# Turning the quantised codes of a feed-forward tile with a transposing DMA instead of TensorE, from tile 14 on

## The reference

```
# attention without softmax, 16 heads of 16: q = elu(xWq+bq)+1, k = elu(xWk+bk)+1, k /= |k|
scores = einsum('bhqd,bhkd->bhqk', q, k);  attn = einsum('bhqk,bhkd->bhqd', scores, v)
x = layernorm(x + (layernorm(x + attn @ Wo + bo) * gamma + beta))

def fp4_quant_dequant(x):            # blocks of 16 along the last dim
    scale = max(max(abs(xb)) / 6, 1e-12)
    xn = xb / scale                  # rounded to 0, .5, 1, 1.5, 2, 3, 4, 6 with its sign
    return rounded(xn) * scale
def fp4_linear(x, w): return fp4_quant_dequant(x) @ fp4_quant_dequant(w).T
h = silu(fp4_linear(x, w_gate)) * fp4_linear(x, w_up)      # w_gate, w_up: 704 x 256
x = layernorm(x + fp4_linear(h, w_down))                   # w_down: 256 x 704
```

## Time and profile before

| | |
|---|---|
| median of 3 runs (lowest, highest) | 700.19 us (700.13, 703.07) |
| the profiled execution, whole | 700.59 us |
| its span, first to last instruction | 698.9 us |
| outside the span | 1.7 us |
| busy share PE / DVE / ACT / POOL | 98% / 84% / 70% / 87% |

### The profile page before, as it was taken

How to read it: one execution, slowest core, us unless ns; L and a number is a source line. 1 busy time by engine, 2 the same in 40 slices (tenths; PEclk the granted TensorE clock), 3 DMA queues, 4 the chain that set the end, 5 groups by cost and what they waited for, 6 DMA issues and landing times.

```text
span 698.9 us, 14240 instructions
## 1 busy us (share of the span) xinstructions
PE 683.4 (98%) x4370; PEld 602.8 (86%) x4370; DVE 584.1 (84%) x1441; ACT 489.3 (70%) x954; POOL 608.8 (87%) x947
## 2 busy tenths in 40 slices
PE   8999999999989999999999999999999999999995
PEld 6888888888868799999999999999999999999995
DVE  6678678876778899889989998998998998998774
ACT  4677777766777676777677677677767767767664
POOL 3988898988888998899989989899899988989766
PEclk9999999999999999999999999999999999999999
DMA  8544443344301111122211122122111211100001
GB/s 267 189 136 136 136 140 117 131 157 155 107 32 34 58 47 46 45 78 75 76 66 57 36 86 80 57 76 76 46 61 62 77 45 47 61 17 16 21 28 45
DMA packets 23135, 56.36 MB, mean 81 GB/s; under 512 B 2642, under 2 KB 5908, under 8 KB 23060
## 3 DMA queue, kind: packets, MB, share of 16 engines
q1 hardware_dynamic: 22640, 55.32, 23.4%
q10 hardware_dynamic: 420, 0.13, 0.1%
HBM read 30.22 MB, written 25.17 MB: 79 GB/s over the span
## 4 chain that ended last, share of the span: by engine, by line
PE 91%; DVE 2%; POOL 2%; issue 2%; ACT 1%; DMA 1%; SPq 0%; POOLq 0%; DVEq 0%
PE banks L407 23%; PE banks L408 22%; PE banks L409 22%; PE banks L553 8%; PE banks L524 7%; PE banks L445 2%; PE banks L418 2%; PE banks L567 1%; PE banks L566 1%; PE banks L431 1%; PE banks L476 1%; DMA arena<-in_L_attn_x_dram 1%; PE banks L484 1%; POOL arena L1164 1%; DVE actT_lo L958 0%
## 5 line engine op out<-in xcount | busy, mean ns | idle before, releaser
L407 PE MATMUL banks<-wgu_hi,actT_lo 128*128 128x512 f32 (+1 forms) x384 | 149.8, 390 | 1.6 <-DVE actT_lo L958 1.4
L408 PE MATMUL banks<-wgu_lo,actT_hi 128*128 128x512 f32 (+1 forms) x384 | 144.0, 375 | 0.0
L409 PE MATMUL banks<-wgu_hi,actT_hi 128*128 128x512 f32 (+1 forms) x384 | 143.3, 373 | 0.0
L725 ACT ACTIVATE arena<-banks 128x512 f32<-128x512 f32 x64 | 38.4, 600 | 111.8 <-PE banks L409 111.6
L1164 POOL TENSOR_TENSOR arena<-arena 128x960 f32<-128x960 f16 (+2 forms) x68 | 115.3, 1695 | 0.0
L1140 POOL TENSOR_TENSOR arena<-arena 128x704 f32<-128x704 f32 x64 | 91.8, 1434 | 20.5 <-DVE arena L945 18.6
L407 PE MATMUL banks<-wd_hi,actT_lo 128*128 128x256 f32 x320 | 100.1, 313 | 0.0
L958 DVE TENSOR_TENSOR actT_lo<-banks,actT_hi 128x512 fp32r<-128x512 f32 (+1 forms) x132 | 85.5, 674 | 16.9 <-ACT actT_hi L711 16.2
L409 PE MATMUL banks<-wd_hi,actT_hi 128*128 128x256 f32 x320 | 90.2, 282 | 0.0
L408 PE MATMUL banks<-wd_lo,actT_hi 128*128 128x256 f32 x320 | 90.2, 282 | 0.0
L407 PEld LDWEIGHTS banks<-wgu_hi,actT_lo 128*128 128x128 f32 x384 | 72.5, 189 | 11.2 <-DVE actT_lo L958 2.3
(11 more groups left out here) (126 smaller groups left out, 1917.3 us busy)
## 6 DMA issues: line engine op xcount, KB each, us to landing
xs<-x_plus_scratch SPq DMA_DIRECT2D x32, 512.0 KB, 3.3
x_plus_scratch<-xs SPq DMA_DIRECT2D x24, 512.0 KB, 2.9
arena<-in_L_attn_x_dram SPq DMA_DIRECT2D x32, 256.0 KB, 3.5
out_dram<-arena SPq DMA_DIRECT2D x32, 256.0 KB, 2.1
x_plus_scratch<-arena SPq DMA_DIRECT2D x4, 512.0 KB, 2.9
x_plus_scratch<-resid SPq DMA_DIRECT2D x4, 512.0 KB, 2.6
resid<-in_L_attn_x_dram SPq DMA_DIRECT2D x4, 256.0 KB, 3.9
resid<-in_L_ffn_w_down_dram SPq DMA_DIRECT2D x1, 704.0 KB, 8.0
```

What stands on the lines that cost most here:

```text
L407: nc.tensor.matmul(dst, sl, mh, start=(k == 0), stop=False, skip_group_check=shared)
L408: nc.tensor.matmul(dst, sh, ml, start=False, stop=False, skip_group_check=shared)
L409: last = nc.tensor.matmul(dst, sh, mh, start=False, stop=(ended and k == n - 1), skip_group_check=shared)
```

## The change

From joint tile 14 on (`BY_DMA = 14`, 54 joint tiles), TensorE no longer transposes the dequantised values. Instead SP issues one transposing DMA that turns the 16-bit codes from `vqc` into `codes` (`turn_codes`). The codes now cover 1024 columns, since the doubled 64 columns are made by ACT before rounding. The scales of a turned tile differ by partition group and by row, so they have to be spread: TensorE transposes the 60 scales (`scales_turn`), ACT copies them out (`scales_copy`), SP writes them to DRAM by three DMAs and reads them back with each row repeated for 16 partitions (`spread_scales`, 512 KB). POOL multiplies turned codes and spread scales (`dequantise_turned`). ACT makes the high parts from that, and copies the multiplied values into two PSUM banks (`high_turned`), from where DVE subtracts the high parts (`low_turned`). `codes` lies in the space of `wo_sb`, the spread scales in tiles 0 to 7 of `resid`; the reloading of x moves to tiles 8 to 15 of `resid` and to later steps.

The core of the diff:

```
+        def by_dma(n):
+            return joint(n) and n >= BY_DMA
-        X_AGAIN = {14 + 8 * i: DEFER + i for i in range(NP - DEFER)}
+        X_AGAIN = {21 + 6 * i: DEFER + i for i in range(NP - DEFER)}
...  SP, at the end of step(t)
+                if by_dma(t + 2):
+                    turn_codes(t + 2)
+                if by_dma(t + 3):
+                    spread_scales(t + 3)
+
+            def turn_codes(n):
+                sp.wait_ge(round_s, n + 1)
+                sp.wait_ge(deq_s, n)
+                sp.dma_start_transpose(codes, vqc[n % 2].bitcast(U16)).then_inc(codes_in, 16)
+
+            def spread_scales(n):
+                i = n - BY_DMA
+                sp.wait_ge(sT_s, i + 1)
+                after(sp, s_each_in[n % 2], 16 * (i // 2))
+                whole = (VC - 1) * GC
+                sp.dma_start(s_turned[n % 2, :, 0:VC - 1, :].rearrange("g c t -> c g t"),
+                             sT[0:whole, :]).then_inc(sT_out, 16)
+                half = GC // 2
+                for k in range(2):
+                    sp.dma_start(s_turned[n % 2, k * half:(k + 1) * half, VC - 1, :],
+                                 sT[whole:whole + half, :]).then_inc(sT_out, 16)
+                sp.wait_ge(sT_out, 3 * 16 * (i + 1))
+                if i < 2:
+                    sp.wait_ge(r3_s, 4 * i + 4)
+                sp.wait_ge(deq_s, n - 1)
+                sp.dma_start(s_each[n % 2].rearrange("p c n -> p (c n)"),
+                             s_turned[n % 2].rearrange("g c t -> g (c t)").unsqueeze(1).broadcast_to(
+                                 [GC, BLK, VC * P])).then_inc(s_each_in[n % 2], 16)
...  PE
+            def scales_turn(n):
+                pe.wait_ge(scale_s, n + 1)
+                pe.wait_ge(r3_s, n - 7)
+                nc.tensor.transpose(ps[0:VB, scales_bank(n), 0:P], s14[:, n % 2, :], ident[:, :]).then_inc(sT_ps, 1)
...  in down(t)
+                if by_dma(t + LAG + 2):
+                    pe.wait_ge(sT_s, t + LAG + 3 - BY_DMA)
...  in step(t)
-                if joint(t + 1):
+                if by_dma(t + 3):
+                    scales_turn(t + 3)
+                if joint(t + 1) and not by_dma(t + 1):
                     turn(t + 1)
+                if by_dma(t + 1) and there(t + 9):
+                    attend(t + 9)
                 if there(t):
                     gate_up(t, 2)
...  ACT
+                if by_dma(n):
+                    nc.scalar.activation(vqb[n % 2][:, RN, 0:RW].bitcast(F16), halves(vy[:, n % 2, VW - RW:VW]), ACT.Copy,
+                                         scale=F16_ONE)
...
+            def scales_copy(n):
+                act.wait_ge(sT_ps, n - BY_DMA + 1)
+                after(act, sT_out, 3 * 16 * (n - BY_DMA))
+                nc.scalar.activation(sT[0:VB, :], ps[0:VB, scales_bank(n), 0:P], ACT.Copy).then_inc(sT_s, 1)
+
+            def high_turned(n):
+                act.wait_ge(deq_s, n + 1)
+                if there(n - 2):
+                    act.wait_ge(gu_ps, 3 * n - 3)
+                act.wait_ge(dn_ps, n - 1 - LAG)
+                a, v = chunks(n)[0], v_turned(n)
+                nc.scalar.activation(vT_hi[:, n % 2, a:VC - 1, :], v[:, a:VC - 1, :], ACT.Copy).then_inc(vT_hi_s, 1)
+                nc.scalar.activation(vT_hi[:, n % 2, VC - 1, :], v[:, VC - 1, :], ACT.Copy,
+                                     scale=upper[:, :]).then_inc(vT_hi_s, 1)
+                act.wait_ge(vT_lo_s, n)
+                nc.scalar.activation(v_in_banks(a), v[:, a:VC, :], ACT.Copy).then_inc(v_ps, 1)
...  ACT's step(t) begins with high_turned(t + 1), ahead of silu(t, 0); scales_copy(t + 3) stands where high(t + 1) stood
...  DVE
+            def low_turned(n):
+                a = chunks(n)[0]
+                dve.wait_ge(vT_hi_s, 2 * n + 2)
+                dve.wait_ge(v_ps, n - BY_DMA + 1)
+                nc.vector.tensor_tensor(vT_lo[:, n % 2, a:VC, :], v_in_banks(a), f32(vT_hi[:, n % 2, a:VC, :]),
+                                        ALU.subtract).then_inc(vT_lo_s, 1)
...  POOL
+            def dequantise_turned(n):
+                a = chunks(n)[0]
+                pool.wait_ge(codes_in, 16 * (n - BY_DMA + 1))
+                pool.wait_ge(s_each_in[n % 2], 16 * ((n - BY_DMA) // 2 + 1))
+                pool.wait_ge(vT_lo_s, n - 1)
+                nc.gpsimd.tensor_tensor(v_turned(n)[:, a:VC, :], codes[:, a:VC, :].bitcast(F16), s_each[n % 2][:, a:VC, :],
+                                        ALU.mult).then_inc(deq_s, 1)
```

More of the change, by code:

```diff
@@ L54, in build @@
     x_plus = nc.dram_tensor("x_plus_scratch", (NP, P, 4 * D), F32, kind="Internal").ap()
+    GC = P // BLK
+    s_turned = nc.dram_tensor("scales_scratch", (2, GC, VC, P), F32, kind="Internal").ap()
     with ExitStack() as ctx:
@@ L166, in f32, with v_turned, v_in_banks, scales_bank @@
             return a.bitcast(F32)
-        x_again, xs_again, rows_again = (resid[:, a:b, :] for a, b in ((0, 2), (2, 6), (6, 8)))
+        x_again, xs_again, rows_again = (resid[:, a:b, :] for a, b in ((8, 10), (10, 14), (14, 16)))
         xs_again = xs_again.rearrange("p (j k) d -> p j k d", j=2)
+        BY_DMA = 14
+        codes = wo_sb[:, :, :].rearrange("p k d -> p (k d)").bitcast(U16).rearrange("p (c n) -> p c n", c=VC)
+        s_each = [resid[:, 4 * i:4 * i + 4, :].rearrange("p t d -> p (t d)").rearrange("p (c n) -> p c n", c=VC)
+                  for i in range(2)]
+        def v_turned(n):
+            return va[:, (n + 1) % 2, :].rearrange("p (c n) -> p c n", c=VC)
         ps = ctx.enter_context(nc.psum_tensor("banks", [P, 8, 512], F32))
+        def v_in_banks(a):
+            return ps[:, 4:6, :].rearrange("p b (c n) -> p (b c) n", n=P)[:, a:VC, :]
+        def scales_bank(n):
+            return DN_BANK[n % 2]
         X_BANK, KV_ACC, KV_BANK, Q_BANK = 0, 1, 2, 6
@@ L208, in build @@
         vT_ps, vT_hi_s, vT_lo_s = sem("vT_ps"), sem("vT_hi"), sem("vT_lo")
+        sT_ps, sT_s, sT_out, codes_in = (sem(n) for n in ("scales_turned", "scales_copied", "scales_out", "codes_in"))
+        v_ps = sem("v_in_banks")
+        s_each_in = [sem(f"scales_in{i}") for i in range(2)]
         gu_ps, g_act, h_s = sem("gu_ps"), sem("g_act"), sem("h_done")
@@ L574, in step @@
                     gate_up(t, 1)
-                if joint(t + 1):
+                if by_dma(t + 3):
+                    scales_turn(t + 3)
+                if joint(t + 1) and not by_dma(t + 1):
                     turn(t + 1)
+                if by_dma(t + 1) and there(t + 9):
+                    attend(t + 9)
                 if there(t):
                     gate_up(t, 2)
-                if there(t + 9):
+                if not by_dma(t + 1) and there(t + 9):
                     attend(t + 9)
@@ L749, in step @@
             def step(t):
+                if by_dma(t + 1):
+                    high_turned(t + 1)
                 if there(t):
@@ L757, in step @@
                     ln3_apply(t - 6, t)
-                if joint(t + 1):
+                if by_dma(t + 3):
+                    scales_copy(t + 3)
+                if joint(t + 1) and not by_dma(t + 1):
                     high(t + 1)
@@ L1017, in step @@
                     aggregate(1, t, have + n3 + n1 + 1)
-                if joint(t + 1):
+                if by_dma(t + 1):
+                    low_turned(t + 1)
+                elif joint(t + 1):
                     low(t + 1)
@@ L1173, in step @@
                     ln1_affine(t + 7)
-                if joint(t + 2):
+                if by_dma(t + 2):
+                    dequantise_turned(t + 2)
+                elif joint(t + 2):
                     dequantise(t + 2)
```

11 lines of the change are left out of this document (7 added, 4 removed).

## The result

The changed kernel takes 831.03 us (median of 4 runs, 828.25 to 834.07) against 701.31 us before (4 runs): 1.1848 times as long, 95% interval 1.1783 to 1.1913. The forecast was 827 us. The profiled execution has a span of 831.9 us.

A forecast was written before the change was run, and what follows sets the result against it. TensorE bounds the kernel now, DVE and POOL close behind; afterwards a loop through the transposing DMA, 4.6 us + L per joint tile. The sum 557.2 + 54 L gives 827 us at L = 5.0; range 773 to 892, 8 in 10: 732 to 955.

The forecast's parts named there:

- TensorE's 0.87 us a step: Second phase: eight transposes (0.99 us) give way to one of the scales (0.12), so TensorE's step falls to 6.7 us.
- The floor of POOL: POOL's own work in a regular step with the new product: 7.26 to 7.61 us, against a step of 7.58 now.
- the best case: Rival: the DMA is fast (L under 3.0) and POOL sets the step; 696 us (690 to 704), chance 0.09.
- that loop: Once per joint tile: cut, transposing DMA, POOL's product, joint_scales, residual, with handovers; 4.6 us + L, 9.6 a step.
- L: Time from SP's issue of the transposing DMA to POOL's release: taken as 5.0 us, ends 2.1 and 9.1.
- 557.2 + 54 L: Whole kernel time in us, from 53 periods of 4.6 + L plus start, end and corrections; 827 at L = 5.0.
- The loop without L: Per joint tile: cut 0.67, handovers, POOL's product 2.3, joint_scales 0.70, residual 0.33; sum 4.6 us.
- the handovers: Waits between engines in each joint tile's loop: 0.2 us each to SP, POOL and DVE.
- The way of the scales: Four DMAs to DRAM and back, some 6 us, needed a period later; priced at nothing unless landing takes 9 us or more.
- The crawl: Rival: transposing DMA moves or issues blocks one after another, L over 6.2; 935 us at 7, 1043 at 9; chance 0.22.
- the nearly covered DMA: Rival: transposing DMA as a plain copy, L 3.1 to 4.0, loop 7.7 to 8.6, time 725 to 773 us; chance 0.19.

The follow-up runs named there:

- The run with both loops open and free scales: Changed kernel with joint_scales' wait loosened, the turn first in SP's steps, and the spread read left out for all but two turned tiles: 697.1 us.
- the run with the loosened wait: Changed kernel, but joint_scales waits for over_scales and the scales' transpose two tiles back, not the dequantisation: 834.2 us, ratio 1.189.
- 754.5: Changed kernel with joint_scales' wait loosened, turn first in SP's steps, read in 16 rows, and scales transposed and copied earlier: 754.5 us, ratio 1.074.

## Why the prediction was right, and where it was wrong

- *Right: what bounds the kernel, and what would bound it next.* TensorE's 0.87 us a step could not be collected. The floor of POOL was put at 7.26 to 7.61 us a step and the best case at 696 us (690 to 704). The run with both loops open and free scales gave 697.1 us, with regular steps of 7.26 us and POOL busy for 98% of them.
- *Right in part: that a DMA between `cut` and the product in the same step makes every step wait.* The waits are where the forecast put them, in POOL, DVE and ACT, and the next turn follows POOL's start by a nearly fixed time. But that loop does not hold the step at 9.7 us: opened by itself it gained nothing, and left closed with the read out of the way it gave 727 us.
- *The number is in good part luck: terms of the sum were off and cancelled.* With the measured L the forecast's own sum, 557.2 + 54 L, would be 874 us. The loop without L was 4.6 us and measured 3.68: the handovers take 0.02 to 0.1 us of it instead of 0.6 (POOL's product ends at 518.22 and DVE starts at 518.33), the product takes 2.15 instead of 2.3, and `cut` hands over 0.44 us after its start, not 0.67. L was 5.0 and measured 5.86. Sum 9.6 forecast; 9.73 measured, in which the reloading of x adds more than forecast: in eight steps, those with DVE's eight additions for it, the rest is 5.3 to 5.7 us instead of 3.68, which is 14 us in all, not 4.4. Only a third of that is the additions. In the same eight steps `cut` itself takes 1.21 to 1.45 us instead of 0.41: it starts some 0.6 us later, beside POOL's 704-column product (L1243), and ends about 0.3 us behind that. No run tests whether the neighbour is the reason; at 960 columns, ahead of the turned tiles, `cut` took 0.64 us beside the same product.
- *Wrong: "The way of the scales ... I price it at nothing".* This is the step that failed. The read of the scales costs 104 us by itself: it stands in the queue ahead of every turn, and it is the longest piece of a second loop, two steps long, that holds the step at 9.6 us without the first. The forecast had asked whether the scales arrive in time, not what they stand in front of. In L it had put a plain copy at 4.0 us, which lands after 2.4, and had added 1 us for small blocks and this queue together; it is 0.7 for turning and 2.2 for the queue (a landing of 5.3 against 3.1). So the 5.0, too, came near by two errors against each other.
- *Wrong in size: what the engines do in a step.* TensorE is busy for 79% of a step, 7.7 us at a granted clock of 0.89, not for about 70% or 6.7 us; ACT for 6.5 us, not 7.2.
- *Wrong: L as a property of the DMA.* The sum 557.2 + 54 L treats it as given. In the run with the loosened wait, the turn was issued sooner and L grew by just as much. L is a landing time in a queue that other waits feed; for the turn alone it is 3.1 us to landing, and 3.2 to 3.4 to POOL's start.
- *Rivals.* The crawl and the nearly covered DMA are out: the turn alone would be nearly covered, as that rival said, and the queue takes it out of reach. The Trainium skill's rule that a transposing DMA is as fast as a regular one (Advanced Engine Details and Errata, X-Bar Transpose (TRN2)) is nearly true here: 3.1 against 2.4 us. The Trainium skill's 1309 ns for a 128x128 piece (VectorE: DVE Perf Modes, The three transpose paths) does not scale to eight pieces: 10.5 us by the estimate of eight times that, 3.1 measured.
- *Open:* what the lower clock of TensorE adds (in the run with the loosened wait nothing of the chain between 300 and 800 us is TensorE, at a clock of 0.94 over the span, against 0.92 here), and the rest between 754.5 and 697 us, where POOL still waits for the codes behind a read that is shorter but there.

## What to carry to other kernels

Before moving work to DMA, write down the loop it enters, then write down every other DMA in the same queue and what each stands in front of; a read that arrives in time can cost 104 us by delaying the one behind it. When one wait is removed and nothing changes, look for a landing time that grew by what was won: another loop, through the queue, holds the step and has to be shortened first. Here the loosened wait was worth nothing with the read in place, and 13 us without it. Check the floor of the second busiest engine first: here it left 0.6% to win at the most.

## What the runs showed of the hardware that was not expected

- A DMA that transposes 128x1024 16-bit values from SBUF to SBUF lands after 3.1 us (median, the 512 KB read left out), a plain copy of the same 256 KB after 2.4; SP is occupied 1.26 us instead of 0.53 to issue it.
- With the DMA engines busy for 91% of the time instead of 21%, ten steps took 75.80 us as before, and DVE, ACT and POOL were busy for no longer.
- The same 512 KB read out of 16 rows, each repeated 8 times, instead of 8 rows repeated 16 times, landed after 4.8 us instead of 6.7 and made the kernel 28 us faster, with twice as many small writes.
- A 256 KB store that landed in 2.1 us before lands in 6.6 behind such reads, while SP's issue of it grew only from 0.34 to 0.47 us.
- `cut`, 1024 16-bit columns from SBUF to SBUF on DVE, took 0.41 us in most steps, and 1.21 to 1.45 us in the eight where it began beside POOL's 704-column product.
